# Gate scores of a mixture-of-experts kernel: the transposed rows as the stationary operand, the 8 gate columns moving

## The reference

```python
xn = _layernorm(x, axis=-1)
...
scores = xf @ gate_w.T                       # xf: 8192 x 512, gate_w: 8 x 512
scores = (jnp.tanh(scores) + 1.0) * 0.5
vals, idx = jax.lax.top_k(scores.T, k)       # k = 1024
kept_w = vals.T
...
o = o * kept_w[:, :, None]
out = xf.at[flat_idx].add(o.reshape(k * n, d))
```

## Time and profile before

| | us |
|---|---|
| median of 3 runs | 2631.4 |
| the profiled execution, its own time | 2631.34 |
| its span, first to last instruction | 2629.4 |
| PE busy in the span | 2600.1 (99%) |
| DVE busy | 2080.6 (79%) |
| ACT busy | 1461.9 (56%) |
| POOL busy | 683.2 (26%) |

### The profile page before, as it was taken

How to read it: one execution, slowest core, us unless ns; L and a number is a source line. 1 busy time by engine, 2 the same in 40 slices (tenths; PEclk the granted TensorE clock), 3 DMA queues, 4 the chain that set the end, 5 groups by cost and what they waited for, 6 DMA issues and landing times.

```text
span 2629.4 us, 38805 instructions
## 1 busy us (share of the span) xinstructions
PE 2600.1 (99%) x11590; PEld 2107.3 (80%) x11592; DVE 2080.6 (79%) x3582; ACT 1461.9 (56%) x2504; POOL 683.2 (26%) x1006
## 2 busy tenths in 40 slices
PE   8999999999999999999999999999999999999998
PEld 4588888888888888888788888888888888888886
DVE  8778888888888888888877778878788787887754
ACT  5744555555555555555545555565555655556553
POOL 5422222222222222223523214113142231411102
PEclk9999999999999999999999999999999999999999
DMA  9733222233333222235447436364363643636313
GB/s 374 259 128 113 79 89 87 88 104 112 112 113 112 84 93 83 89 102 170 138 137 187 109 116 158 92 157 130 115 158 91 157 130 115 159 91 157 98 55 72
DMA packets 262638, 329.62 MB, mean 125 GB/s; under 512 B 142032, under 2 KB 142160, under 8 KB 258640
## 3 DMA queue, kind: packets, MB, share of 16 engines
q1 hardware_dynamic: 228816, 230.91, 28.1%
q0 software_dynamic: 33664, 96.75, 15.0%
HBM read 259.14 MB, written 68.45 MB: 125 GB/s over the span
## 4 chain that ended last, share of the span: by engine, by line
PE 85%; DVE 9%; issue 3%; ACT 1%; DMA 1%; POOL 0%; SPq 0%; DVEq 0%; POOLq 0%; ACTq 0%
PE ring L1590 9%; PE ring L1591 9%; PE ring L1592 9%; PE po L2570 6%; PE po L2572 6%; PE po L2571 6%; PE pb L2572 4%; PE pb L2571 4%; PE pb L2570 4%; PE po L1628 4%; PE po L1629 4%; PE po L1630 4%; PE pc L2572 2%; PE pc L2570 2%; PE pc L2571 2%
## 5 line engine op out<-in xcount | busy, mean ns | idle before, releaser
L2570 PE MATMUL po<-w2h,hid_h 128*128 128x512 f32 x1024 | 399.2, 390 | 2.1 <-DVE hid_l L2507 1.2
L1590 PE MATMUL ring<-xt_h,w_h 128*128 128x512 f32 x1024 | 400.1, 391 | 0.1
L1591 PE MATMUL ring<-xt_l,w_h 128*128 128x512 f32 x1024 | 398.6, 389 | 0.0
L2571 PE MATMUL po<-w2l,hid_h 128*128 128x512 f32 x1024 | 398.4, 389 | 0.0
L1592 PE MATMUL ring<-xt_h,w_l 128*128 128x512 f32 x1024 | 398.4, 389 | 0.0
L1379 DVE SCALAR_TENSOR_TENSOR u<-xin,cw,u 128x512 f32<-128x512 f32 x384 | 288.5, 751 | 73.5 <-issue 44.7
L2047 POOL DMA_INDIRECT out_dram<-res,idx_c x64 | 109.0, 1703 | 488.1 <-DVE res L2417 477.1
L2570 PEld LDWEIGHTS po<-w2h,hid_h 128*128 128x128 f32 x1024 | 192.2, 188 | 44.9 <-DVE hid_l L2407 3.8
L1590 PEld LDWEIGHTS ring<-xt_h,w_h 128*128 128x128 f32 x1024 | 192.2, 188 | 41.0 <-DVE xt_l L543 0.9
L1592 PEld LDWEIGHTS ring<-xt_h,w_l 128*128 128x128 f32 x1024 | 192.2, 188 | 40.1
L2571 PEld LDWEIGHTS po<-w2l,hid_h 128*128 128x128 f32 x1024 | 192.2, 188 | 39.9
(11 more groups left out here) (299 smaller groups left out, 6234.0 us busy)
## 6 DMA issues: line engine op xcount, KB each, us to landing
w2r<-fc_in SPq DMA_DIRECT2D x256, 256.0 KB
wo<-wo_halves POOLq DMA_DIRECT2D x120, 512.0 KB, 4.4
w1r<-fc_in SPq DMA_DIRECT2D x144, 256.0 KB
x_tail<-x_in SPq DMA_DIRECT2D x64, 256.0 KB, 2.8
out_dram<-res SPq DMA_DIRECT2D x64, 256.0 KB, 2.0
g_x<-x_in SPq DMA_DIRECT2D x15, 1024.0 KB, 9.3
xt_rows<-g_xnt SPq DMA_DIRECT2D x15, 1024.0 KB, 10.9
rows<-xt_rows SPq DMA_DIRECT2D x15, 1024.0 KB, 6.1
```

The costliest lines, as they stand in the source:

```text
L1590: pe.matmul(ring[r % 2][:, :], w_h[:, r, q], xt_h[:, k, :], start=(k == 0), stop=False)
L1591: pe.matmul(ring[r % 2][:, :], w_h[:, r, q], xt_l[:, k, :], start=False, stop=False)
L2570: pe.matmul(dst, ah, bh, start=start, stop=False, skip_group_check=more)
L2571: pe.matmul(dst, ah, bl, start=False, stop=False, skip_group_check=more)
```

## The change

The two operands of the gate's matmul change places. For each slice k and each quarter j of the block's rows, the 128 x 128 piece of `xnt` is stationary and the 8 gate columns move, so that the product comes out as 128 rows x 8 columns and four quarters stand side by side, 128 x 32, as the tanh needs them. `sc_t`, its copy on ACT and the four small transposes are gone, together with their two semaphores and the leftover in the mixer. The two banks take turns for even and odd blocks. The tanh of block b - 1 stays where it was on ACT, behind the copies of block b, and now waits for the matmuls themselves.

```diff
-    pst = banks[6][0:E, :]
-    psc = banks[7][:, 0:J * E]
+    psc = [banks[6 + i][:, 0:J * E] for i in range(2)]
...
-    def turn_scores(pe, b):
-
-        pe.wait_ge(c_sr, b + 1 + 1)
-        pe.wait_ge(c_ta, b + 1)
-        pe.sem_inc(t_tick, 1)
-        for j in range(J):
-            last = pe.transpose(psc[:, j * E:(j + 1) * E], sc_t[:, j * P:(j + 1) * P],
-                                ident[0:E, 0:E])
-        last.then_inc(c_sc, 1)
-
-    def turn_tanh(act, b):
-        act.wait_ge(c_sc, b + 1 + 1)
+    def scores_tanh(act, b, i):
+        act.wait_ge(c_se, (b + 1) * KD + 1)
         act.wait_ge(c_v, b * 2 + 1)
-        act.activation(tanh[:, :], psc, ACT.Tanh).then_inc(c_ta, 1)
+        act.activation(tanh[:, :], psc[i % 2], ACT.Tanh).then_inc(c_ta, 1)
...
-                if not (first and i == 0):
-                    turn_scores(pe, b - 1)
-                pe.wait_ge(c_sr, b + 1)
+                if not (first and i < 2):
+                    pe.wait_ge(c_ta, b - 1 + 1)
                 for k in range(KD):
                     pe.wait_ge(c_tc, b * KD + k + 1 + 1)
-                    pe.matmul(pst, gw[:, k, :], xnt[i][:, k, :], start=(k == 0),
-                              stop=(k == KD - 1)).then_inc(c_se, 1)
+                    for j in range(J):
+                        last = pe.matmul(psc[i % 2][:, j * E:(j + 1) * E], xnt[i][:, k, j * P:(j + 1) * P],
+                                         gw[:, k, :], start=(k == 0 and j == 0),
+                                         stop=(k == KD - 1 and j == J - 1))
+                    last.then_inc(c_se, 1)
...
-                act.wait_ge(c_se, (b + 1) * KD + 1)
-                act.wait_ge(c_sc, b + 1)
-                act.copy(sc_t[:, :], pst).then_inc(c_sr, 1)
...
             for c in range(NC_):
                 in_step(b, c)
-                if c == 0 and first_turn:
-                    end_scores(pe)
```

More of the change, by code:

```diff
@@ L271, in stage_gate @@
     gv = ew.gamma[:, :].rearrange("p (n e) -> p n e", e=E)
-    sc_t = m.sb("g_sc_t", [E, TB])
     tanh = m.sb("g_tanh", [P, J * E])
@@ L296, in stage_gate @@
     c_se = sums.c_scores
-    c_sr = m.count("g_sr")
-    c_sc = m.count("g_sc")
     c_win = sums.c_small_in
@@ L304, in stage_gate @@
     p_tick, d_tick = ends.p_tick, ends.d_tick
-    t_tick = m.tick("g_ttick")
     c_id = m.count("g_id")
@@ L350, in end_values @@
         gate_values(dve, NB - 1)
-    def end_scores(pe):
-        turn_scores(pe, NB - 1)
     def end_tanh(act):
-        turn_tanh(act, NB - 1)
+        scores_tanh(act, NB - 1, R - 1)
     def sync(sp):
@@ L616, in group @@
                 if not (first and i == 0):
-                    turn_tanh(act, b - 1)
+                    scores_tanh(act, b - 1, (i - 1) % R)
                 if not (last and i == R - 1):
@@ L630, in scalar @@
         group(NG - 1, last=True)
-    return sync, gpsimd, vector, tensor, scalar, end_store, end_values, end_scores, end_tanh
+    return sync, gpsimd, vector, tensor, scalar, end_store, end_values, end_tanh
 class Experts:
@@ L1004, in stage_mixer @@
     rows_out = (pb, pc)
-    end_store, end_values, end_scores, end_tanh = gate_ends
+    end_store, end_values, end_tanh = gate_ends
     po, c_o, c_po = ends.po, ends.c_o, ends.c_po
```

## The result

The changed kernel took 2689.85 us (median of six executions, 2676.08 to 2695.63), the kernel before 2631.59 us beside it. The ratio is 1.0206 (95% interval 1.0191 to 1.0221): 2% slower, 58 us. I had forecast no change, at 2630.1 us; what came is the first rival, the clock, which I had given 0.36.

A forecast was written before the change was run, and what follows sets the result against it. PE, DVE and DMA were all taken as full mid-stage, so only the ends gain: 0.3 (last blocks) + 0.35 (last block's copy) + 0.54 (mixer) = 1.2 us off 2631.34, forecast 2630.1 us. Range 2626.5 to 2712, the case's own 2628.5 to 2631.5.

The forecast's parts named there:

- the first rival, the clock: Gate stage: without wide matmuls TensorE stays at 1.2 GHz, 2709 us, or about 2670 back and forth; chance 0.36.
- the term for the clock: Gate stage: the forecast assumed loads of the stationary operand keep the clock up, so it added nothing.
- The argument against the rival: Gate stage: PE is never idle for long, and the trace's only clock fall follows pure idleness, so no fall.
- The PE's block at the full clock: Gate stage, per block: 1.89 transposes + 3.52 narrow matmuls + 0.1 turn = 5.51 us, 0.26 less than before.
- the turn: PE, each gate block: going from narrow matmuls back to transposes was estimated to add 0.1 us.
- The second rival: Gate stage: loads don't overlap in a long run, 2.3 us more per block, 2665 us; chance 0.04.
- The middle of the stage: Middle gate blocks: DVE (5.64 us) and full DMA hold them, so the PE's saving gives 0, at most 1.3 us.
- The last block: Gate block 15: without the scores' copy, ACT starts its copies 0.75 us after the transposes instead of 1.10, saving 0.35 us.
- the leftover's 0.54 us: Mixer: the four leftover small transposes disappear from the PE's path, saving 0.54 us.
- The rival's price: Gate stage at 1.2 GHz: 48 loads at 0.2175 us, 10.8 us per block with turns, 5.0 more; +78 us in all.
- The third rival: Gate stage: PE held it, DVE's loop shortens and transfers keep up, so 4.8 us less, 2626.5 us; chance 0.05.

The follow-up runs named there:

- move64: Changed kernel with each narrow matmul moving the 8 gate columns eight times over (64 columns): 2632.35 us, ratio 1.0002 to the kernel before.
- half_wide: Kernel before with two of the four wide matmuls per block left out, so half the features don't enter the scores: 2631.47 us, ratio 0.9998.
- move128: Changed kernel with the 8 gate columns repeated sixteen times (128 columns moving in each narrow matmul): 2631.25 us, ratio 0.9996 to the kernel before.
- again: Changed kernel run once more with no edit: 2691.86 us median, ratio 1.0209 to the kernel before; its profiled execution took 2694.51 us.

## Why the prediction was wrong

The step that failed is the choice between the forecast and its first rival, that is, the term for the clock, which the forecast put at nothing. "If loads of the stationary operand keep the clock up, nothing happens": they don't. With loads in all of the stage the mean clock was 0.59 and 0.50, and blocks took 7.01 to 10.13 us where the forecast had kept 5.77. The argument against the rival, that the changed stage "is never idle for long, and the only fall in this trace comes after pure idleness", weighed an absence: no stretch of the kernel before had the PE busy with few columns moving, so its trace could not speak for either side.

The rival came true, but not all that I gave for it did. I read in the earlier trace rows that wide matmuls brought the clock up and transposes alone had not yet. In the changed kernel's first block nothing but transposes runs ahead of 12.28 us, and the 32 passes behind them take 3.73 us, 0.117 each; at 29.41 the clock is up behind transposes again, 0.51 and then 0.96. So transposes do raise it here, and it is the narrow passes behind which it falls. This differs from the rule of the Trainium skill that the prediction quotes ("TensorE: Matmul & The Clock Gate", "Part 4: PE-mode transpose"), and the measurement decides. The fall at 33 us without a gap is also one that the section "Why this matters for your kernels" of that page of the Trainium skill, by which the stage would have stayed at 2.4 GHz, doesn't cover.

- The PE's block at the full clock: worked out 5.51 us, 5.32 in a full stream in move64 (17.77 to 23.09). A pass was 0.11 us (19.57 to 23.09 for 32), as L1649's loads said; the 0.1 us for the turn wasn't there and the transposes took 1.80. The second rival, loads that don't overlap, was wrong.
- The middle of the stage gains nothing from a shorter PE block: right, shown by half_wide.
- The last block: ACT begins its copies 0.74 us behind the transposes in move64 (101.76 and 102.50), where 0.75 was taken. The mixer's twelfth matmul and the next are 0.23 us apart in move64 (109.92 and 110.15), so the leftover's 0.54 us are gone. But the mixer's first matmul is at 107.30 there, where I looked for 106.5, and at 1281.50 the PE waits 1.39 us for DVE, where the kernel before waits for nothing (1280.59); ahead of it DVE had waited 2.53 us for a gather of gates, against 1.19. The totals are level with before, 2631.25 us in move128, not 1.2 us less; that is below what the runs can tell.
- The rival's price: 10.8 us were worked out for a slow block and 10.13 measured. The passes ran 0.209 us apart, where I used the 0.2175 of the first transposes, and the turns cost less. For a stage slow throughout I wrote 2709 us and again has 2694.5; for one back and forth 2670, and the profiled execution has 2676.
- The third rival, that the gain arrives, needed DVE to get shorter, and it did not until its work was moved.

Open: why executions of one program fall into one pattern of the clock or the other. Four of the six executions behind the result report a mean clock of 0.989 or 0.990 and yet took 2688 to 2696 us, longer than the two with 0.977; there is no trace of one of them. Why the same transposes are followed by a rise early in the stage and not later is open too.

## What to carry to other kernels

When a matmul's operands change places so that the small one moves, the work may fit the same time by its loads and still run at half the clock, with next to no idle time to warn of it: look for what keeps columns moving in that stage before counting instructions. If the small operand has to move, repeat its columns up to what fits under a load, which cost nothing here and took 58 us off. And a trace in which something never occurs is no evidence against it; price such a rival by the rows that come nearest.

## What the runs showed of the hardware

- TensorE's clock fell to 1.2 GHz at about 33 us of the first profiled execution with PE and PEld busy throughout (0.96, then 0.53), and stayed there (0.50) in another where both were busy for 130.00 of 130 us. With 8, 32, 64 and 128 moving columns in otherwise equal kernels, the medians were 2690, 2675, 2632 and 2631 us.
- With 8 columns moving, a load of 128 x 128 in float32 and its pass follow the last ones after 0.117 us at a clock of 0.93 and after 0.209 us at 0.50; with 64 columns, after 0.11 us at 1.00.
- The clock rose behind transposes alone: 0.51 in them, 0.96 in the passes behind them.
- More work can be faster: two wide matmuls more per block took 24 us off.
- A DVE instruction that takes 0.66 us in another profile took 3.71 us beside two of POOL, and the PE waited 1.22 us for it.
